# Four graph layers on one core: pair products in runs of two, and one ring for masked scores and probabilities

## What is computed

```python
# layer 0: one head, scores from two vectors
e = leaky_relu(s1[:, :, None] + s2[:, None, :]); att = softmax(where(adj > 0, e, -9e15)); x = ln(x + elu(att @ h))
# layer 1: 8 heads of 32, a feed-forward part behind it
scores = einsum('fnhd,fmhd->fhnm', q, k) / sqrt(D); attn = softmax(where(mask, scores, -1e9))
t = einsum('fhnm,fmhd->fnhd', attn, v); x = ln1(x + t); x = ln2(x + relu(x @ w1 + b1) @ w2 + b2)
# layer 2: 4 heads, as layer 0.  layer 3: one head
e = leaky_relu(einsum('bnd,bmd->bnm', x @ W1, x @ W2)); x = ln(x + relu(softmax(where(adj > 0, e, -1e12)) @ (x @ W3)))
```

## Time and profile before

| | |
|---|---|
| device time, median of 3 runs | 2945.64 us (2944.88 to 2947.49) |
| the profiled execution's device time | 2947.72 us |
| its span, first to last instruction | 2945.9 us |
| busy: PE, DVE, ACT, POOL | 93%, 88%, 90%, 80% |

### The profile page before, as it was taken

How to read it: one execution, slowest core, us unless ns; L and a number is a source line. 1 busy time by engine, 2 the same in 40 slices (tenths; PEclk the granted TensorE clock), 3 DMA queues, 4 the chain that set the end, 5 groups by cost and what they waited for, 6 DMA issues and landing times. The chain is left out here.

```text
span 2945.9 us, 69361 instructions
## 1 busy us (share of the span) xinstructions
PE 2746.8 (93%) x22356; PEld 1518.6 (52%) x22576; DVE 2579.1 (88%) x8261; ACT 2655.0 (90%) x5079; POOL 2350.2 (80%) x2517
## 2 busy tenths in 40 slices
PE   5899999999999999999999999999999999999865
PEld 4344445555555555555555555555555555554433
DVE  6678889888999999999999999898999989999764
ACT  6668989889999999999999999999999999998964
POOL 5467779778888888888888888888888888887774
PEclk8999999999999999999999999999999999999978
DMA  7345567667767767777776766676677677666564
GB/s 174 69 94 109 106 114 145 124 118 144 136 132 136 139 134 137 135 133 132 138 140 135 137 135 135 128 140 136 133 140 139 132 133 140 135 126 124 107 114 92
DMA packets 1215804, 378.91 MB, mean 129 GB/s; under 512 B 1157712, under 2 KB 1194320, under 8 KB 1215440
## 3 DMA queue, kind: packets, MB, share of 16 engines
q1 hardware_dynamic: 1213616, 373.46, 67.5%
q10 hardware_dynamic: 1824, 0.99, 0.2%
HBM read 21.43 MB, written 16.78 MB: 13 GB/s over the span
## 5 line engine op out<-in xcount | busy, mean ns | idle before, releaser
L991 POOL TENSOR_TENSOR split_r<-prob_r,split_r 128x512 f16<-128x512 f32 x768 | 882.5, 1160 | 297.7 <-DVE split_r L1466 292.9
L1430 DVE CUSTOM_DVE_ANT_0 unused<-bank_ps,neg_mask 128x512 bf16<-128x512 f32 x1024 | 664.2, 684 | 70.5 <-PE bank_ps L1642 69.5
L1708 PE MATMUL bank_ps<-val_r,trans_r 128*128 128x64 f16 (+1 forms) x9216 | 636.0, 221 | 66.9 <-DMA trans_r<-split_r 63.0
L1708 PEld LDWEIGHTS bank_ps<-val_r,trans_r 128*128 128x128 f16 x9216 | 528.3, 98 | 267.6 <-issue 88.4
L1235 ACT ACTIVATE prob_r<-bank_ps 128x512 f32<-128x512 f32 x1024 | 581.6, 621 | 30.6 <-PE bank_ps L1660 18.4
L1214 ACT ACTIVATE prob_r<-masked_r,low_r 128x512 f32<-128x512 f32 x768 | 537.7, 728 | 38.3 <-DVE low_r L1415 31.0
L1668 PE MATMUL bank_ps<-prob_r,value_ones 128*64 128x512 f32 (+1 forms) x2048 | 540.0, 609 | 5.6 <-ACT prob_r L1235 0.8
L1415 DVE CUSTOM_DVE_ANT_0 masked_r<-bank_ps,neg_mask 128x512 f32<-128x512 f32 x768 | 511.4, 684 | 35.6 <-ACT bank_ps L1203 28.1
L1466 DVE TENSOR_SCALAR_CACHE_REDUCE split_r<-prob_r 128x512 f16<-128x512 f32 x768 | 512.2, 677 | 33.8 <-ACT prob_r L1214 22.4
L1659 PE MATMUL bank_ps<-stack 98*128 98x512 f16 x1024 | 392.4, 383 | 13.4 <-DVE low_r L1415 4.4
L1203 ACT ACTIVATE bank_ps<-spread_r,near 128x512 f32<-128x512 f32 x512 | 345.4, 702 | 12.7 <-DVE low L1430 7.5
(11 more groups left out here) (148 smaller groups left out, 4664.1 us busy)
## 6 DMA issues: line engine op xcount, KB each, us to landing
stack<-qk SPq DMA_DIRECT2D x384, 128.0 KB, 2.5
xcur<-in_x_dram SPq DMA_DIRECT2D x32, 512.0 KB, 3.9
out_dram<-z SPq DMA_DIRECT2D x32, 512.0 KB, 3.4
trans_r<-split_r SPq DMA_TRANSPOSE x768, 3.3
xt_r<-split_r SPq DMA_TRANSPOSE x320, 3.3
stack<-low_rows SPq DMA_DIRECT2D x128, 4.0 KB
qk<-in_adj_dram SPq DMA_DIRECT2D x1, 1024.0 KB, 7.9
z<-in_L_gnn_W_dram SPq DMA_DIRECT2D x4, 256.0 KB, 12.2
```

What stands on the lines that cost most here:

```text
L991: nc.gpsimd.tensor_tensor(split_r[:, j, 1, :], prob_r[:, i, :], split_r[:, j, 0, :], ALU.subtract).then_inc(lo_done.sem, 1)
L1430: nc.vector.tensor_tensor_reduce(out=unused[:, nth % 2, :], in0=bank_ps[entry("bank", "sq", g, t, b, h)][:], in1=neg_mask[:, b, :], scale= ...
L1708: ins = nc.tensor.matmul(bank[:, at:at + width], trans_r[:, i, pp, jb, :], val(g, layer)[:, vp, jb, cols], start=(n == 0), stop=(n == len( ...
```

## The change

Three things are changed.

1. `PW_RUN` goes from 0 to 2. In `settle()` the pair products of key blocks 0 and 1, and of 2 and 3, of one pair of heads get the later one's planned start, so that they stand one behind the other. `NUDGE` and `OFFSET` are added to that, each product's own, and can part them again.
2. `masked_r` (4 entries) is gone and `prob_r` has 11. The mask writes into the entry of `prob_r`, and the exponential works in place. The wait for a free entry moves from ACT's exponential (`ex`) to DVE's mask (`mk`). `schedule()` still plans with 4 and 7; `settle()` hands out 11.
3. `NUDGE` and `OFFSET` are new tables. On each engine about half of the tasks move, by 1 to 11 places. `EARLY`, the first four splits of rows at the start, now follows POOL's order.

```diff
+    IN_RING = {"masked": "prob"}
+    RINGS = {**POOLS, "prob": 11}
...
-    NUDGE = {"add_0": -1.4, "add_1": 1.5, "add_3": -0.1, "ap_0": 0.5, "ap_2": 1.6, "ap_3": 0.7, "ap_ffn": -0.2, "ap_out": -0.3,
+    NUDGE = {"add_0": 0.2, "add_1": -4.7, "add_3": -1, "ap_0": -1.8, "ap_1": -1.9, "ap_2": -0.4, "ap_3": 2.3, "ap_ffn": 0.1,
...
-    PW_RUN = 0
+    PW_RUN = 2
...
-            for entry in closes:
-                closers.setdefault(entry, []).append(key)
+            for name, opener in closes:
+                closers.setdefault((IN_RING.get(name, name), opener), []).append(key)
...
-        entries = {name: [[-1e18, None, n] for n in range(size)] for name, size in POOLS.items()}
+        entries = {name: [[-1e18, None, n] for n in range(size)] for name, size in RINGS.items()}
...
             for name, opener in tasks[key][3]:
+                name = IN_RING.get(name, name)
...
-        masked_r = sb("masked_r", [P, POOLS["masked"], N])
-        low_r = sb("low_r", [P, POOLS["masked"]])
-        prob_r = sb("prob_r", [P, POOLS["prob"], N])
+        low_r = sb("low_r", [P, RINGS["prob"]])
+        prob_r = sb("prob_r", [P, RINGS["prob"], N])
...
-        EARLY = [("x", g, 0, n) for g in range(2) for n in range(CT)]
+        EARLY = [("x", *key) for kind, *key in ORDER["pool"] if kind == "x_lo"][:2 * CT]
...
                 elif kind == "ex":
-                    was = prior("prob", *unit)
-                    if was is not None:
-                        act.wait_ge(*prob_free(was))
                     act.wait_ge(*masked_done.at(*unit))
-                    i = entry("masked", *unit)
-                    nc.scalar.activation(prob_r[:, entry("prob", *unit), :], masked_r[:, i, :], ACT.Exp,
+                    i = entry("prob", *unit)
+                    nc.scalar.activation(prob_r[:, i, :], prob_r[:, i, :], ACT.Exp,
...
-                    i = entry("masked", *unit)
-                    was = prior("masked", *unit)
+                    i = entry("prob", *unit)
+                    was = prior("prob", *unit)
                     if was is not None:
-                        dve.wait_ge(*probs_done.at(*was))
+                        dve.wait_ge(*prob_free(was))
                     dve.wait_ge(*leaky_done.at(*unit))
-                    nc.vector.tensor_tensor_reduce(out=masked_r[:, i, :], in0=bank_ps[entry("bank", "sc", *unit)][:],
+                    nc.vector.tensor_tensor_reduce(out=prob_r[:, i, :], in0=bank_ps[entry("bank", "sc", *unit)][:],
```

More of the change, by code:

```diff
@@ L122, in graph_layers_kernel @@
     SHIFT = {}
-    NUDGE = {"add_0": -1.4, "add_1": 1.5, "add_3": -0.1, "ap_0": 0.5, "ap_2": 1.6, "ap_3": 0.7, "ap_ffn": -0.2, "ap_out": -0.3,
[4 rows of a table removed]
-             "job_hi_k": -3.3, "job_hi_s2": -1.4, "job_hi_v": 0.2, "job_k": -1, "job_lo_c0": 0.2, "job_lo_f2": 0.2, "job_lo_g":
[9 rows of a table removed]
-    OFFSET = {0: 0.1, 1: 0.4, 2: 1, 3: -0.2, 4: 0.9, 8: -0.4, 9: 0.5, 11: 0.1, 12: 0.6, 14: -0.3, 16: 0.7, 17: 0.2, 18: -0.8,
[32 rows of a table removed]
+    NUDGE = {"add_0": 0.2, "add_1": -4.7, "add_3": -1, "ap_0": -1.8, "ap_1": -1.9, "ap_2": -0.4, "ap_3": 2.3, "ap_ffn": 0.1,
[14 rows of a table added]
+    OFFSET = {0: -12.5, 1: 1, 2: 1.7, 3: 2.6, 4: -0.4, 9: -0.5, 10: -0.5, 11: -1, 12: -0.3, 13: 0.3, 14: -0.8, 15: -0.4, 16:
[33 rows of a table added]
     DRIFT = {}
-    PW_RUN = 0
+    PW_RUN = 2
     STEP = {"add_0": 1.22, "add_1": 1.23, "add_3": 1.23, "ap_0": 0.97, "ap_1": 0.99, "ap_2": 0.98, "ap_3": 0.98, "ap_ffn": 0.98,
```

## The result

The changed kernel takes 2927.33 us (median of 4, 2925.5 to 2927.97) against 2945.26 us before (4 runs, 2941.66 to 2947.49): the ratio is 0.9939, with a 95% interval of 0.9927 to 0.9951, so 18 us less, 14 to 22. The forecast was 2920 us, 26 less. The two profiled executions are 20.4 us apart, by their spans.

The account below looks back on a forecast made before the run. PE's stream was taken to bound the kernel: 28 us shorter, less 3 lost at start and end, plus 1 from the ring, nothing for run waits or moved times, gave 2945.6 - 26 = 2920 us, range 2898 to 2942.

Parts of the forecast that it names:

- What bounds the kernel: Middle of the kernel: PE, 97.7% busy, sets the pace; time taken from its stream should show if ACT, 95.4%, follows.
- The prices of a run's edges: PE's steps: two pair products take 1.87 us, one alone 1.00; entry 0.31, leaving square scores 0.33; each array change about 0.1.
- Leaving, entering, square scores: PE's stream: 24 us less for leaving runs, 11 less for entering, 7 more at square scores; together 28 us shorter.
- What a run waits for: Pair products at L1668: first product held for the second's exponentials; costed at nothing, 136 us at the very most.
- One ring of 11: Ring waits at exponentials and mask: gain of 1 us taken, from 0 to 12.6; masks' new waits taken as 0.
- Times moved anew: Tasks moved by 1 to 11 places on each engine: taken as 0, with 22 us either way as ends.
- A: Whole PE stream: half of the 26 us gain becomes waiting as ACT's chains run late; 2933 us, chance 0.18.
- B: PE's middle: moved times and looser ring also clear half of 44 idle us; 2898 us, chance 0.17.
- C: Mask at L1415: masks wait for the shared ring and DVE becomes the bound; 2973 us, chance 0.09.
- D: Run edges on PE: runs save nothing and only the ring's 1 us comes; 2945 us, chance 0.06.
- The check I named: Signs of being right: pair products at 1.86 to 1.87 us, 85.3 us a graph, PE about 97.5%, ACT over 96%.

Follow-up runs that it names:

- e4: The changed kernel with the separate rings of 4 and 7 tiles again, same runs and planned times: 2970.2 us, 1.0091 of before.
- e6: The kernel before with only the joint start of a run's products, one shift per run, rings of 4 and 7, old times: 3049.4 us, 1.0365 of before.
- e8: The changed kernel with its 71 lone pair products put in runs as well, by one shift per run: 2940.2 us, 0.9988 of before.
- e7: The kernel before with the shared ring of 11 and the joint start, one shift per run, old planned times: 3001.1 us, 1.0198 of before.
- e9: e7 with turned scores from the fifth of an unbroken row on, if the run doesn't need them, done behind the run: 3016.4 us, 1.0256 of before.
- e11: Runs and ring of 11, PE keeping e7's order with old times, the other engines taking the changed kernel's new times: 3094.9 us, 1.0519 of before.
- e2: The kernel before with only the new NUDGE and OFFSET, no joint start, rings of 4 and 7: 3043.8 us, 1.0345 of before.
- e3: The changed kernel with PW_RUN back at 0, so no joint start, keeping new tables and ring of 11: 3040.0 us, 1.0329 of before.
- e5: The changed kernel with PE doing the task behind a run of two between its two products: 3006.2 us, 1.0215 of before.
- e1: The kernel before with only the shared ring of 11, old runs and planned times: 2937.1 us, 0.9988 of before.
- e10: e7 with every run planned 1.0 us earlier: 3052.0 us, 1.0377 of before.

## Why the prediction was right, and by how much it was off

**What bounds the kernel.** PE is 98% busy in the middle, before and after, with ACT close behind at 95.7%, and the gain came where PE's stream got shorter. But the stream alone does not set the time: in e4 it is that of the changed kernel, in e6 to e8 it is shorter than that of before, and e4, e6 and e7 are slower than before all the same. In e9 to e11 ACT waits 60, 101 and 150 us for turned scores, against 37 in e7.

**The prices of a run's edges.** 1.86, 1.00, 0.31 and 0.33 us are the medians in all fourteen traces, whatever the order, but for the runs of two in e2 and e3 (2.33 and 2.22 us). Adding up the smallest steps of each kind in the two traces, PE's stream in the middle went from 1834.7 to 1817.3 us, 17.4 less; with finer kinds it is 20. Of the forecast 28 us over 32 graphs, 19 belong to these 22, so the stream came out as forecast. The two rules of the Trainium skill part here: "TensorEngine Tiling (Array Packing)", "Key Properties", says that a change of the tiling mode drains the engine, and the 0.1 us at each such change agree. "TensorE: Matmul & The Clock Gate" of the Trainium skill, "The mechanism" in Part 3, lets a weight load overlap only where the group of rows differs, though the same section also names a background weight buffer. The 0.22 us between full-width products and 1.863 us for two pair products don't agree with the first, which the prediction quoted alone.

**Leaving, entering, square scores.** The three terms (24, 11 and -7) could not be measured each for itself. e5 puts 215 runs back and costs about 81 us, of which the terms explain 43.

**What a run waits for: nothing.** Right: PE's wait for pair exponentials at L1668 is 0.4 us in the changed kernel, 1.4 without the ring (e4) and 5.5 with the old times (e7). What this term looked past is what a held product does elsewhere. It keeps exponentials in the ring, which without the shared ring makes the kernel 45 us slower (e4), and it moves the turned scores together, which with the old times makes it about 75 us slower (e7); the one shift for each run may be some 14 of these, by e8.

**One ring of 11: 1 us.** Right in size for the ring alone (e1, 1 to 6 us). As a part of the change it was mis-sized: the sum valued it by the waits of a kernel without runs. Masks waiting for the ring, which I took at 0, waited 1.9 us. ACT's copy of the pair sums, which asks for an entry of the ring too, is not in the prediction at all, and it waits 14.8 us.

**Times moved anew: 0.** The two ends named, 22 us either way, were far too narrow as bounds of what order can do: e7 and the changed kernel differ by 2.6% in it. The net value that I took was near: waits in the middle, counted from starts, went from 62.4 to 68.0 us, 5.6 more, or 9 more with finer kinds of steps. This is the term that was mis-sized, and by it the middle lost 12 us and not 19. That it came so near 0 is luck: the zero stood for "nothing tells which", while the three parts had been fitted to each other, and any two of them without the third lose 27 us or more against before (e4, e3 and e7). The rest of the kernel gave 8.4 us where 6 were forecast; e1 has its few us there too, without runs.

**The rivals.** A (half of the gain turns to waiting) came nearest in size besides the forecast: 18 us of 26 are kept. Its mechanism, chains just in time that are now late, is what the middle shows, at less than half of the gain. B did not come: the transfers' waits that it would have cleared are still about 19 us. C did not come with 11 tiles. D is refuted by the steps of the 219 runs.

**The check I named.** Runs at 1.86 to 1.87 us: yes. A graph 0.9 us shorter: 0.54 over 22 graphs, 0.7 over the 11 of the earlier trace rows. PE about 97.5%: 98.0. ACT over 96%: 95.7.

**A rival that no run tests.** The new tables fit only the kernel with runs (e2, e3). No run has tables made anew for the kernel without them, so it is not shown that such tables alone could not give 0.6% too. What the traces do show is where this gain came from: the stream got shorter, and the waits did not.

## What to carry to other kernels

Where a tuned order, a buffer and a grouping are changed together, price the grouping by its steps in the trace (their medians held to 0.01 us), but don't value the parts by the waits of the old kernel: the ring was worth 0.12% without runs and 1.5 to 1.7% with them, and the runs cost 2% with the old times and paid only with new ones. When two engines are both over 95% busy, moving one kind of task by a us can cost more than the grouping gains (e10), so group tasks in the planner and then let it place everything anew. Ask of every user of a buffer what it will wait for, the rare ones too: here the wait moved to a copy that runs four times a graph. And before a wait called "issue" is taken for a riddle, look at what PE's weight load waited for at the same place. And measure over an even number of periods where two alternate.

## What was not expected of the hardware

The two heads' float32 products run side by side only if both are ready: a run of two took 2.96 us instead of 1.87 when a head's exponential came late (e3), a cost that appears mostly as PE busy and not as a wait (574.7 us in L1668 against 540.0 before, where the products stand in almost as many runs). How much of the new tables' worth lies in which engine stays open.
